# Routing statistics and gate logits inside the first attention's program, and the first experts' first layer as three fp16 part products

## The reference

```
x = x + attention0(layernorm(x), ctx, mask)         # 16 heads of 64, keys and values from ctx
x = x + experts0(layernorm(x))                      # 8 experts, each takes the 256 tokens it scores highest
x = x + attention1(layernorm(x), ctx)               # 16 heads of 16, a band of 128 tokens
x = x + experts1(layernorm(x))                      # 8 experts in 4 groups
```

```
xf = layernorm(x)                                   # 2048 x 256
scores = (tanh(xf @ gate_w.T) + 1) * 0.5            # 2048 x 8
vals, idx = top_k(scores.T, 256)                    # per expert, 256 tokens
y = layernorm(xf[idx]) * gamma + beta
h = gelu(y @ fc1[e].T + b1[e])                      # 256 -> 1024
o = (h @ fc2[e].T + b2[e]) * vals                   # 1024 -> 256
out = xf with o added to the chosen rows
```

## Time and profile before

| | us |
|---|---|
| median of 3 runs | 1176.66 |
| lowest, highest | 1173.72, 1181.28 |
| the profiled execution's own time | 1175.02 |
| its span (first to last instruction of the profile) | 1173.1 |
| PE busy | 1065.8 |
| DVE busy | 759.5 |
| ACT busy | 676.7 |

### The profile page before, as it was taken

One profiled execution on the slowest core, in us unless ns is written; L12 is line 12 of the kernel. 1 busy time (PEld: TensorE's weight loads), 2 busy tenths in 40 slices (PEclk: granted clock), 3 DMA queues, 4 the chain that ended last, 5 costly groups with the idle time before them and its releaser, 6 DMA issues. The chain is left out here.

```text
span 1173.1 us, 28682 instructions
## 1 busy us (share of the span) xinstructions
PE 1065.8 (91%) x10231; PEld 785.1 (67%) x10232; DVE 759.5 (65%) x2183; ACT 676.7 (58%) x1282; POOL 529.1 (45%) x599
## 2 busy tenths in 40 slices
PE   6999999999999999966699999698998866999996
PEld 3666777767777777666388886344454445888885
DVE  5888888888878877956611116668777774455553
ACT  6878876777768776837232216357667643343331
POOL 4677545465356433310147740566667523233312
PEclk9999999999999999985699999899999977999998
DMA  7633432333333422243546636624444241111110
GB/s 255 167 74 86 88 74 73 92 82 73 76 68 94 93 69 69 62 154 122 172 139 192 187 64 188 187 65 123 139 122 143 61 134 37 29 27 31 27 14 10
DMA packets 120027, 116.16 MB, mean 99 GB/s; under 512 B 43488, under 2 KB 100064, under 8 KB 119776
## 3 DMA queue, kind: packets, MB, share of 16 engines
q1 hardware_dynamic: 112608, 105.27, 31.9%
q0 software_dynamic: 7296, 9.25, 4.7%
HBM read 59.89 MB, written 21.82 MB: 70 GB/s over the span
## 5 line engine op out<-in xcount | busy, mean ns | idle before, releaser
L576 ACT ACTIVATE e<-masked,neg_max 128x512 f32<-128x512 f32 x256 | 184.4, 720 | 47.0 <-DVE neg_max L677 44.2
L651 DVE TENSOR_TENSOR e_t_lo<-et,e_t_hi 128x512 f16<-128x512 f32 x256 | 176.4, 689 | 46.1 <-ACT e_t_hi L569 43.9
L677 DVE CUSTOM_DVE_ANT_0 masked<-sc,mask_bias 128x512 f32<-128x512 f32 x256 | 175.3, 685 | 28.3 <-issue 24.5
L569 ACT ACTIVATE e_t_hi<-et 128x512 f16<-128x512 f32 x256 | 151.2, 591 | 68.3 <-PE et L468 67.0
L468 PEld LDWEIGHTS et<-ident,e 128*128 128x128 f32 x1024 | 124.5, 140 | 57.4 <-issue 8.9
L468 PE MATMUL et<-ident,e 128*128 128x128 f32 x1024 | 154.4, 273 | 1.2 <-ACT e L576 0.8
L2140 ACT ACTIVATE d_e<-d_st 128x384 f32<-128x384 f32 (+1 forms) x192 | 94.0, 526 | 49.4 <-PE d_st L2283 44.6
L70 PE MATMUL ob<-v_hi,e_t_hi 128*128 128x65 f16 x1024 | 119.0, 193 | 1.2 <-issue 1.2
L71 PE MATMUL ob<-v_lo,e_t_hi 128*128 128x65 f16 x1024 | 119.2, 193 | 0.0
L72 PE MATMUL ob<-v_hi,e_t_lo 128*128 128x65 f16 x1024 | 118.4, 193 | 0.0
L70 PE MATMUL h_hb<-h_xt_hi,experts_hi 128*128 128x256 f16 x352 | 96.8, 275 | 3.8 <-DVE h_xt_lo L2514 3.8
(11 more groups left out here) (466 smaller groups left out, 2758.7 us busy)
## 6 DMA issues: line engine op xcount, KB each, us to landing
kk<-nat_k SPq DMA_DIRECT2D x64, 256.0 KB, 3.5
raw<-in_fc SPq DMA_DIRECT2D x16, 1024.0 KB, 7.5
qq<-nat_q SPq DMA_DIRECT2D x64, 128.0 KB, 2.4
qk<-scratch_stack SPq DMA_DIRECT2D x64, 128.0 KB
scratch_stack<-kq_hi SPq DMA_DIRECT2D x16, 256.0 KB, 3.0
scratch_stack<-kq_lo SPq DMA_DIRECT2D x16, 256.0 KB, 3.1
d_expert_raw<-in_gate_w SPq DMA_DIRECT2D x8, 512.0 KB, 3.8
d_expert_raw<-in_up_w SPq DMA_DIRECT2D x8, 512.0 KB, 3.9
```

Source lines behind the costliest of these rows:

```text
L569: nc.scalar.activation(e_t[u % NBUF].hi[:], et[u % 2][:], ACT.Copy).then_inc(turned_hi, 1)
L576: nc.scalar.activation(e[u % NBUF][:], masked[u % NBUF][:], ACT.Exp, bias=neg_max[:, g % 2, j:j + 1], scale=-1.0).then_inc(exp_ok, 1)
L651: nc.vector.tensor_tensor(e_t[u % NBUF].lo[:], et[u % 2][:], e_t[u % NBUF].hi[:], ALU.subtract).then_inc(turned_lo, 1)
L677: nc.vector.tensor_tensor_reduce(masked[u % NBUF][:], sc[j % 2][:], mask_bias[g // PAIRS % 2][:, j % QT, :], -SCALE0, 3e38, ALU.add, ALU.m ...
```

## The change

The first routing's front goes into the first attention. `side_work` gets groups "r": in batch b >= 2, at unit 7 of its first two pairs, PE transposes the normalized x of batch b-2, and at (30, 7) and (31, 3) that of batch 2, 4 transposes each, six groups. ACT normalizes two tiles for each ahead of it, reads the bank out into `T.z_t.hi`, and DVE writes `T.z_t.lo`. `late_statistics` gets a kind "r" of 22 steps for batches 0 to 2, from unit 40 of batches 1, 2 (one step a unit) and 3 (two steps a unit). The gate is loaded and split in fp16 parts (`gate_w`). Behind the last added tile the statistics and transposes of batch 3 follow, in their own chain, and PE makes all logits as three fp16 products of 8 columns (96 of them); tanh goes to `T.route_tanh`. The tables of Sqrt and Tanh are loaded ahead of their use.

`phase_route0` starts with the score. The split of the second attention's weights (`w_lo`), `r_eighth` and `r_column` move behind the search, `wo_lo` behind the keys; POOL writes the first candidates' offsets first.

`phase_experts0` splits each expert's `yt` (ACT `turned_high`, DVE `turned_low`) and its `fc1` (ACT `weights_high`, DVE `weights_low`, two halves each, one buffer `fc1_parts` for all experts), and `first_layer` uses `three_products`: 48 matmuls instead of 16 fp32 products. SP loads `fc1` of expert e as soon as the low parts of expert e-2 stand.

```diff
+    if j == 7 and b >= 2 and p < 2:
+        return "r", (b - 2, p)
+    if (g, j) in LAST_ROUTE:
+        return "r", (B - 2, LAST_ROUTE.index((g, j)))
...
+def late_steps(u):
+    b, at = u // (PAIRS * UNITS), u % (PAIRS * UNITS)
+    step, route = at - LATE_AT, at - ROUTE_AT
...
+    if b >= 1 and route >= 0:
+        steps = (route,) if b + 1 < B else (2 * route, 2 * route + 1)
+        return [("r", b - 1, n) for n in steps if n < ROUTE_STEPS]
...
+                pe.wait_ge(turned_lo, units)
+                pe.wait_ge(gate_lo, 1)
+                for t in range(NT - QT):
+                    route(t)
+                for i in range(2):
...
+                    for t in range(2):
+                        for c in range(DT):
+                            mm = pe.transpose(route_banks[i][:, c * 2 + t, :], early_z[2 * i + t][:, c * P:(c + 1) * P], T.ident[:])
+                    mm.then_inc(z_turned, 1)
+                for i in range(2):
+                    pe.wait_ge(z_lo, 2 + i + 1)
+                    for t in range(2):
+                        mm = route(NT - QT + 2 * i + t)
...
-                statistics(0)
-                statistics(1)
-                for b in range(B):
-                    normalize(b)
-                    if b + 2 < B:
-                        statistics(b + 2)
...
                 for e in range(2, E):
-                    sp.wait_ge(h_full, GR * (e - 1))
+                    sp.wait_ge(fc1_lo, DT * (e - 1))
                     W.load1(sp, dram, e)
...
+                def turned_high(e):
+                    act.wait_ge(affine, e + 1)
+                    if e >= 2:
+                        act.wait_ge(h_full, GR * (e - 1))
+                    nc.scalar.activation(yt_parts[e % 2].hi[:], yt[e % 2][:], ACT.Copy).then_inc(yt_hi, 1)
+
+                def weights_high(e):
+                    act.wait_ge(W.fc1_in[e % 2], 16 * (e // 2 + 1))
+                    if e >= 1:
+                        act.wait_ge(h_full, GR * e)
+                    for c in range(DT):
+                        nc.scalar.activation(fc1_parts.hi[:, c, :], W.fc1[e % 2][:, c, :], ACT.Copy).then_inc(fc1_hi, 1)
...
+                    if e + 1 < E:
+                        turned_high(e + 1)
+                        weights_high(e + 1)
...
                         scale_turned(e + 1)
+                        turned_low(e + 1)
+                        weights_low(e + 1)
                     if e >= 1:
                         weigh(e - 1)
...
                 def first_layer(e):
-                    pe.wait_ge(W.fc1_in[e % 2], 16 * (e // 2 + 1))
-                    pe.wait_ge(affine, e + 1)
+                    pe.wait_ge(yt_lo, e + 1)
+                    pe.wait_ge(fc1_lo, DT * (e + 1))
...
-                                mm = pe.matmul(hb[n % 2][:, i, :], W.fc1[e % 2][:, c, f * P:(f + 1) * P], yt[e % 2][:, c, :], start=(c == 0), stop=(c == DT - 1))
+                                mm = three_products(pe, hb[n % 2][:, i, :], (fc1_parts.hi[:, c, cols], fc1_parts.lo[:, c, cols]),
+                                                    (yt_parts[e % 2].hi[:, c, :], yt_parts[e % 2].lo[:, c, :]), c == 0, c == DT - 1)
```

More of the change, by code:

```diff
@@ L117 @@
 GROUP0, COPY0, ADD0, DIRECT0, ORDER0 = number_groups()
+LATE0 = {step: n for n, step in enumerate(step for u in range(PAIRS0 * UNITS) for step in late_steps(u))}
+EXPERTS0 = 8
+GATE_AT = 41
 EARLY = ("ctx0", "wk_a", "wq_a", "wv_a")
@@ L629, in _ @@
                         high_part(SPLIT_AT0[u])
-                    ahead = side_work(u // UNITS, u % UNITS + 2) if u < units and u % UNITS == 3 else None
+                    if u == GATE_AT:
+                        act.wait_ge(gate_in, 16)
+                        nc.scalar.activation(gate_w.hi[:], gate_raw[:], ACT.Copy).then_inc(gate_hi, 1)
+                    ahead = side_work((u + 2) // UNITS, (u + 2) % UNITS) if u + 2 < units else None
+                    if ahead is not None and ahead[0] == "r":
+                        b, i = ahead[1]
+                        act.wait_ge(late_ok, LATE0["r", b, ROUTE_STEPS - 1] + 1)
+                        act.wait_ge(pj_full, GROUP0["w", (b, QT - 1)] + 1)
+                        for t in range(2):
+                            route_norm(late_z[b % 2][i][:, t, :], b, 2 * i + t)
                     if ahead is not None and ahead[0] == "z":
                         b, i = ahead[1]
-                        act.wait_ge(late_ok, b * LATE_STEPS)
+                        act.wait_ge(late_ok, LATE0["z", b, LATE_STEPS - 1] + 1)
                         if b >= 3:
@@ L637, in _ @@
                             norm(late_z[(b - 1) % 2][i][:, t, :], b * QT + 2 * i + t)
+                act.wait_ge(exp_ok, units)
+                nc.scalar.activation(warm, T.ident[:, 0:1], ACT.Sqrt)
                 act.wait_ge(last_turned, 1)
                 nc.scalar.activation(last_part.hi[:, CT - 1, :], last_bank[:], ACT.Copy).then_inc(last_hi, 1)
+                root(2, sd2)
+                act.wait_ge(shift_ok, 2)
+                for t in range(2, QT):
+                    route_norm(early_z[t], B - 1, t)
+                for i in range(2):
+                    act.wait_ge(z_turned, 2 + i + 1)
+                    cols = slice((B - 1) * S + i * 2 * P, (B - 1) * S + (i + 1) * 2 * P)
+                    nc.scalar.activation(T.z_t.hi[:, :, cols], route_banks[i].rearrange("p (c t) n -> p c (t n)", c=DT), ACT.Copy).then_inc(z_hi, 1)
+                nc.scalar.activation(warm, T.ident[:, 0:1], ACT.Tanh)
+                act.wait_ge(logits, 1)
+                nc.scalar.activation(T.route_tanh[:], logit, ACT.Tanh)
             @block.vector
@@ L1409, in phase_experts0 @@
         yt = [sb(f"yt{i}", [P, DT, CAP]) for i in range(2)]
+        yt_parts, fc1_parts = [Split(sb, f"yt{i}", [P, DT, CAP]) for i in range(2)], Split(sb, "fc1", [P, DT, FF0])
         h = [sb(f"h{i}", [P, FT0, CAP]) for i in range(2)]
@@ L1419, in phase_experts0 @@
         keys_full, consts = sem("fkeys_full"), sem("fconsts")
+        yt_hi, yt_lo, fc1_hi, fc1_lo = (sem("f" + n) for n in ("yt_hi", "yt_lo", "fc1_hi", "fc1_lo"))
         gathered = [sem(f"fgathered{i}") for i in range(2)]
@@ L1541, in weigh, with turned_low, weights_low @@
                                                             in1=wb2[e % 2][:, n, :], op0=ALU.mult, op1=ALU.add).then_inc(res_ok, 1)
+                def turned_low(e):
+                    dve.wait_ge(yt_hi, e + 1)
+                    nc.vector.tensor_tensor(yt_parts[e % 2].lo[:], yt[e % 2][:], yt_parts[e % 2].hi[:], ALU.subtract).then_inc(yt_lo, 1)
+                def weights_low(e):
+                    for c in range(DT):
+                        dve.wait_ge(fc1_hi, DT * e + c + 1)
+                        nc.vector.tensor_tensor(fc1_parts.lo[:, c, :], W.fc1[e % 2][:, c, :], fc1_parts.hi[:, c, :], ALU.subtract).then_inc(fc1_lo, 1)
+                weights_low(0)
                 for n in range(KEYS_ROUTE, KEYS_FIRST):
```

289 lines of the change are left out of this document (147 added, 142 removed).

## The result

The changed kernel takes 1169.01 us (median of 5 runs, 1167.03 to 1170.68), against 1176.66 before: a ratio of 0.9934, interval 0.9916 to 0.9952. It is faster by 0.66%, so within 1%. I had said 1154.0 and a range of 1147 to 1163: both were too low. The profiled execution's span fell from 1173.1 to 1165.3, by 7.8 us where 21.6 were forecast. The gap of 13.8 us is laid out here between landmarks that both traces have; each term is the shift of one stretch's length.

What follows compares the result with a forecast made beforehand. PE was taken to bound the first attention and first experts, engines waiting on each other the routing's front. Attention +4.2, front -20.0, behind it +0.2, experts -6.0: -21.6 from 1175.02 gave 1153.4, stated as 1154, range 1147 to 1163.

Steps and rivals of the forecast that it cites:

- Four of them stand in pairs where PE is the bound, 1.8 us on the path: First attention: of six transpose groups at 0.44 us of PE each, four lengthen the path, by 1.8 us.
- A small one takes 0.09: First attention: a small DVE route step takes 0.09 us of the engine, a batch's 22 steps 3.0 us.
- In batches 1 and 2 they lie under PE [...] and cost nothing.: First attention: the small DVE steps fit in 3 us a pair free on DVE, costing nothing in batches 1 and 2.
- The rival at full price (+15): First attention: the added steps cost their full price, +15 us instead of +4.2, giving 1165; chance 0.10.
- The front, -20.0: Routing's front, from the last adds to x: the search begins at about 520.9 instead of 540.87, saving 20.0 us.
- So -7.5: First experts: seven first layers save 1.63 us each, 11.4 in all, less 3.9 for the second one's later start.
- I take the clock as held: First experts: PE's clock survives the 4.5 us pause before the second first layer; if it falls, +2.4 us.
- The first first layer, 588.4 to 594.7: First experts: expert 0's first layer starts 0.8 us late at 588.4, and table load and gelus hold it until 594.7.
- Gathers, "+1.5 (0 to 6)": First experts: rows arrive 13.3 us after a second layer, wanted after 12.6; every second expert waits 0.7, +1.5 us in all.
- The one on clock or gathers: First experts: rival that the clock falls, +2.4 us, or gather transfers take 3.5, +4 more; 1156 to 1160, chance 0.27.
- The store of `r_y`: Before the first gather: rival that this store ends last, 3 us after the token list; 1157, chance 0.10.
- the weights: First experts: rival that `fc1` weights come late and make the kernel slower than before; 1177 or more, chance 0.03.

Runs made afterwards that it cites:

- route_steps_out: Changed kernel without DVE's 22 small route steps for each of batches 0 to 2, scale and shift constant; last batch's first add at 518.15, 3.0 us earlier.
- clock_kept: Changed kernel with 18 unread PE products of 512 columns filling the pause before the second first layer; 1166.62 us, ratio 0.9942.
- the mends: Edits to the changed kernel: expert 1's parts ahead, gathers before scatters, batch 2's route groups behind attention, biases first, expert 1's turn earlier; all together 1154.90 us.
- old_first_layer: Changed kernel with the experts' part of the kernel before (fp32 first layer), all else as changed; 1167.64 us, ratio 0.9946.
- mended_old_layer: Kernel with the mends that do not touch the first layer, but the experts' program of the kernel before (fp32 first layer); 1164.01 us, ratio 0.9907.

## Why the prediction was wrong, step by step

- **"Four of them stand in pairs where PE is the bound, 1.8 us on the path", and 0.5 for the banks.** This is the step that failed most: the six groups cost 6.45 us. I charged a group with PE's 0.44 and a short wait for a bank, the last two with a subtraction on DVE besides, and with no work of ACT. It takes 1.5 us of ACT (two tiles in 0.98, a copy in 0.48 of distance) and 0.62 of DVE, in the order of the units' own work. In the last two pairs a group costs about 1.5 on the path. My own ended one pair too early to show it.
- **"A small one takes 0.09", and 1.9 for the last batch.** The steps took 1.2 of the path there. The price was wrong: see the last section, and the trace of the kernel before had it already, 17 of 39 steps held up. Held-up steps added some 7.5 us to DVE in the r steps, all but 0.4 in batches 1 and 2.
- **"In batches 1 and 2 they lie under PE [...] and cost nothing."** This failed for batch 2: 2.5 us in its last three pairs, where PE was busy for 42.49 of 42.50 us and DVE for 35.53, and DVE got 6 us more. In batch 1 route_steps_out shows 0.1. The rival at full price (+15) did not come.
- **The front, -20.0.** Right, term by term; the table of tanh was the last to end, as said.
- **Behind the front.** Right: `w_lo` is in the gap before the prefix sums.
- **"So -7.5" for the products.** The layer's length was right (5.24, said 5.28), the pause too (5.0, said 4.9). **"I take the clock as held"** failed: +2.3, as its rival priced it. The fall came within a pause of 4.9 us of which 0.7 was PE's work; one idle stretch in the earlier trace rows was too little to call 4.5 us safe.
- **The first first layer, 588.4 to 594.7.** 6.3 was said, 6.5 measured, by luck: the gelu's table load that I let it wait for was over before it began (576.45 to 577.73), and some 12 products at the low clock took its place, about 1.2 us.
- **The Trainium skill's rule** on the slow clock ("TensorE: Matmul & The Clock Gate", Part 1), cited against my choice, agrees with the trace: the clock is 0.51 on the mean for the 4.8 us behind the pause, and clock_kept, where PE is busy 4.05 of the 4.40 us before, has 1.00.
- **Gathers, "+1.5 (0 to 6)".** 3.4 (3.9 by the distance of the starts), inside its bounds. The rows came 14.6 us behind the second layer's end, not 13.3: 0.2 more ahead of the bias, 0.25 more of transfer, and 0.8 because the gather's second call took 1.81 instead of 0.97. Such a hold-up, and a turn at the low clock, also put the first first layer 1.4 late where I had 0.8. The clock's 2.3, some 2.4 here and 0.9 up to the end of the pause are the 5.5 by which the experts missed, to 0.1.
- **Nothing behind the experts.** Wrong by 2.9, of which 2.0 is the bias load's. I had not asked what a stretch full of DMA does when the work around it moves.
- **Rivals.** The one on clock or gathers came true, but alone it would have given 1156 to 1160. The store of `r_y` was issued at 551, long before the first gather; the weights never held PE. But expert 3's landed 2.2 us after ACT was ready for them, and that put DVE's subtraction (615.29) beside the gather call that took 1.81 (615.55). What failed was treating the misses as alternatives: three came together.
- **The sum itself.** 1153.4 was for the profiled execution; with the 1.6 by which the median was higher it would have been 1155.0, not 1154.

What stays open: 0.7 us of the attention; why a group costs 1.2 us in batch 2, 0.65 at the start of batch 3 and 1.5 at its end, and the steps 2.5 in batch 2 but 0.1 in batch 1; and why the bias lands late.

## What to carry over

Price a moved piece of work on every engine that it touches, at the very place where it lands: a pair with little side work had another bound than its neighbours, and engines with time to spare on the mean did not cover small steps everywhere. Before shortening the products of a loop, look at what arrives once a round (gathers, parts, the clock after a pause): what is freed is only paid out when those are earlier too, as old and new first layer with and without the mends show. And in an in-order queue, never put work whose data comes late ahead of work that somebody waits for.

## What the runs showed of the hardware

Small DVE instructions with their data in SBUF are held up by POOL. DVE's and then POOL's rows of the changed kernel:
```profile
250.06 0.86 DVE L814 TENSOR_TENSOR late_words<-route_rstd 128x8 f32<-128x8 f32 x1
252.07 0.65 DVE L816 SCALAR_TENSOR_TENSOR late_words<-late_words 128x8 f32<-128x8 f32 x1
254.40 0.16 DVE L818 SCALAR_TENSOR_TENSOR route_rstd<-late_words,route_rstd 128x8 f32<-128x8 f32 x1
```
```profile
249.78 1.12 POOL L362 TENSOR_TENSOR v_lo<-raw,v_hi 128x512 f16<-128x512 f32 x1
250.84 0.61 POOL L368 CAST o_parts<-o 128x512 f16<-128x512 f32 x1
251.53 1.16 POOL L370 TENSOR_TENSOR o_parts<-o,o_parts 128x512 f16<-128x512 f32 x1
```
The step that begins at 250.06 ends at 250.92, POOL's subtraction at 250.90. Of 81 such steps 31 last over 0.3 us (the others at most 0.22), and each ends 0.01 to 0.03 us behind the end of a CAST or TENSOR_TENSOR of POOL; in the kernel before it is 17 of 39. Statistics and aggregates never are held up. This agrees with the Trainium skill ("SBUF — State Buffer", Who interferes with whom): DVE's second pair of ports is shared with GpSimd, and "it's an exclusive lock".

It goes the other way too: a gather call of POOL takes twice as long beside DVE's subtractions of two SBUF operands.
```profile
569.72 2.01 POOL L1492 DMA_INDIRECT yg<-scratch_y,slot_token  x1 [0.30 <-issue]
572.03 0.95 POOL L1492 DMA_INDIRECT yg<-scratch_y,slot_token  x1 [0.30 <-issue]
```
```profile
568.52 2.36 DVE L1611 TENSOR_TENSOR fc_lo<-raw,fc_hi 128x1024 f16<-128x1024 f32 x2 [1.61 <-ACT fc_hi L1562]
```
The call took 0.98 in all three kernels without `fc_lo` (before, old_first_layer, mended_old_layer), and 1.97 to 2.02 in all eleven that have it. Here the same section of the Trainium skill infers that such a subtraction leaves the generation of descriptors alone. The call as a whole is held; whether it is its descriptors or its reading of the list `slot_token`, no run tells apart.
